# Masks written into the score banks by ScalarE, the up weights split as a seventh part, and new orders and banks in a six-layer local-attention kernel

## The reference

```python
x = attn_layer(shift_tokens(x), Wqkv[i], ...) + x     # 16 heads of 64, windows of 32 tokens
x = ffn_layer(shift_tokens(x), ln_g[i], ..., W1[i], b1[i], W2[i], b2[i]) + x

# attn_layer
q, k, v = split(x @ Wqkv)                  # 128 -> 3 * 1024
q, k = l2norm(q) * qs, l2norm(k) * ksc     # then a rotation by position, scaled
sim = einsum(q, k of this window and the one before) * 8
sim = where(mask, -big, sim)               # mask = (it < jb) | (it > jb + w) | (jb == -1)
return (softmax(sim) @ v) @ Wo
# ffn_layer
xn = layernorm(x) * g + b;  a, gate = split(xn @ W1 + b1)    # 128 -> 2 * 341
return a * gelu(gate) @ W2 + b2
```

## Time and profile before

| | us |
|---|---|
| median of 3 runs | 1497.31 (1495.83 to 1497.71) |
| the profiled execution | 1497.48 |
| its span | 1495.7 |
| PE busy | 1449.7 (97%) |
| DVE busy | 1348.3 (90%) |
| ACT busy | 1275.3 (85%) |
| POOL busy | 1245.6 (83%) |

### The profile page before, as it was taken

The page is one execution under the profiler, slowest core; times in us unless marked ns, Lnnn a source line. Parts: engine busy times, 40 slices in busy tenths (PEclk is TensorE's granted clock), DMA queues, the critical chain, the costliest instruction groups (busy, mean ns, idle before and its releaser), DMA issues.

```text
span 1495.7 us, 67060 instructions
## 1 busy us (share of the span) xinstructions
PE 1449.7 (97%) x26608; PEld 1290.8 (86%) x26608; DVE 1348.3 (90%) x2418; ACT 1275.3 (85%) x2605; POOL 1245.6 (83%) x1214
## 2 busy tenths in 40 slices
PE   6699999999999999999999999999999999999997
PEld 5578898889888888888898888889888988988886
DVE  7699999999999999999999999999999999999974
ACT  4577988888888898898889888888988888888886
POOL 5489988888899889898888898888889888888871
PEclk9999999999999999999999999999999999999999
DMA  6111122111122211221211122121212111211211
GB/s 162 43 42 50 49 59 63 45 49 53 47 54 66 70 37 40 62 63 51 76 43 41 49 57 74 53 61 35 59 36 65 44 45 40 56 49 35 52 46 28
DMA packets 96187, 80.31 MB, mean 54 GB/s; under 512 B 66282, under 2 KB 79598, under 8 KB 95854
## 3 DMA queue, kind: packets, MB, share of 16 engines
q1 hardware_dynamic: 94990, 75.34, 18.8%
q10 hardware_dynamic: 864, 0.26, 0.1%
HBM read 17.91 MB, written 1.05 MB: 13 GB/s over the span
## 4 chain that ended last, share of the span: by engine, by line
PE 88%; issue 4%; DVE 3%; ACT 3%; POOL 1%; DMA 1%; SPq 0%; ACTq 0%; POOLq 0%; DVEq 0%
PE bank L1140 70%; PE bank L1254 11%; PE bank L1292 5%; PE bank L1224 1%; ACT pz L725 1%; DVE parts L944 1%; PE bank L1326 1%; DMA rot<-in_b_v 0%; ACT sq L663 0%; ACT ot L732 0%; DVE n L954 0%; DVE w_lo L1026 0%; DVE s L990 0%; POOL rot L487 0%; POOL rot L476 0%
## 5 line engine op out<-in xcount | busy, mean ns | idle before, releaser
L476 POOL TENSOR_TENSOR rot<-parts 128x512 f32<-128x512 f32 x384 | 492.1, 1288 | 35.4 <-DVE parts L944 33.4
L944 DVE TENSOR_TENSOR parts<-bank,rtab 128x1024 f32<-128x1024 f32 x384 | 458.7, 1200 | 7.7 <-ACT sq L663 7.4
L487 POOL TENSOR_TENSOR rot<-rot,rnorm 128x512 f32<-128x512 f32 x384 | 394.6, 1043 | 12.0 <-DVE rnorm L970 12.0
L493 POOL TENSOR_TENSOR es<-es,r 128x512 f32<-128x512 f32 x192 | 200.4, 1044 | 151.8 <-DVE r L996 151.7
L954 DVE TENSOR_REDUCE n<-sq 128x8 f32<-128x512 f32 x384 | 259.1, 675 | 16.5 <-ACT sq L663 16.5
L1140 PE MATMUL bank<-w_hi,x_hi 128*128 128x512 f32 x576 | 265.6, 461 | 4.0 <-DVE parts L944 2.6
L663 ACT ACTIVATE sq<-bank 128x512 f32<-128x512 f32 x384 | 232.1, 604 | 18.5 <-PE bank L1140 6.9
L725 ACT ACTIVATE pz<-bank 64x512 f32<-64x512 f32 x384 | 225.9, 588 | 5.4 <-PE bank L1292 1.9
L1140 PE MATMUL bank<-w_lo,x_hi 128*128 128x512 f32 x576 | 228.5, 397 | 0.0
L1140 PE MATMUL bank<-w_hi,x_lo 128*128 128x512 f32 x576 | 228.0, 396 | 0.0
L1254 PE MATMUL bank<-ident,rot 128*128 128x128 f32 x1536 | 208.5, 273 | 10.7 <-DVE x_tok L1040 5.0
(11 more groups left out here) (95 smaller groups left out, 2901.9 us busy)
## 6 DMA issues: line engine op xcount, KB each, us to landing
vb<-v SPq DMA_DIRECT2D x96, 384.0 KB, 4.4
w_new<-in_Wqkv SPq DMA_DIRECT2D x36, 256.0 KB, 4.0
vb<-v SPq DMA_DIRECT2D x48, 128.0 KB, 2.3
w_o<-in_Wo SPq DMA_DIRECT2D x12, 256.0 KB
xin<-x_tok SPq DMA_DIRECT2D x48, 64.0 KB
xs<-x_tok SPq DMA_DIRECT2D x48, 64.0 KB, 2.0
xin<-x_tok SPq DMA_DIRECT2D x48, 56.0 KB
xs<-x_tok SPq DMA_DIRECT2D x48, 56.0 KB, 2.3
```

What stands on the lines that cost most here:

```text
L476: g.tensor_tensor(rot[:, i * CH:(i + 1) * CH].rearrange(halves, z=2, c=HD), parts[:, b:b + CH].rearrange(halves, z=2, c=HD), parts[:, b + ...
L487: g.tensor_tensor(c, c, over(r, CHH, DH), ALU.mult).then_inc(s_sc[i], 1)
L493: g.tensor_tensor(e, e, over(r8[:, (u % 2) * PAIRS:(u % 2 + 1) * PAIRS], PAIRS, DH), ALU.mult)\
L944: d.tensor_tensor(parts[:, b:b + 2 * CH].rearrange("p (w h c) -> p w h c", w=2, c=DH), heads(bank[QK_BANK[i]][:, :]).unsqueeze(1).to_broad ...
```

## The change

It has four parts.

1. The eight mask products of each `scores` go. In their place ScalarE copies the mask, now f32, from SBUF into the two score banks before the score products (`seed`, four instructions of 128 x 512 in a step), and the score products accumulate onto it. Before the pipeline starts, TensorE runs one product of 512 columns into each of the banks 2 and 3. Both `S_BANK` entries now use the banks 2 and 3.
2. The up weights are a seventh part in the same chain as the six of `Wqkv`: `next_hi` on ScalarE and `next_lo` on GpSimd, in the seventh of a layer's eight steps that split. `w_new` holds two parts of `Wqkv` by turns and the up weights apart; `w1_hi` and `w1_lo` hold two layers. `up_hi`, `up_lo` and their semaphores go.
3. The order inside `iteration` is new on all five engines, and the banks are new.
4. `align_block` is at the head of TensorE's iteration, with slot 24.

The core of the diff (the written-out orders are shown as they come out of the build below):

```diff
-QK_BANK, T_BANK = (2, 1, 2, 5, 1, 2, 5, 7), (0, 0, 7, 3, 6, 5, 4, 7)
-V_BANK, P_BANK, O_BANK = (3, 6, 5, 0), (4, 6, 7, 4), (2, 6, 7, 4)
-S_BANK, W_BANK, H_BANK = ((6, 3), (3, 1)), (3, 5), (6, 7, 4)
-XIN_BANK, N_BANK, D_BANK = 0, 4, 0
+QK_BANK, T_BANK = (7, 6, 3, 5, 4, 2, 1, 3), (0, 0, 5, 4, 7, 6, 7, 0)
+V_BANK, P_BANK, O_BANK = (2, 5, 1, 0), (7, 1, 7, 1), (5, 6, 4, 4)
+S_BANK, W_BANK, H_BANK = ((2, 3), (3, 2)), (4, 6), (0, 5, 6)
+SEEDED = (2, 3,)
+XIN_BANK, N_BANK, D_BANK = 6, 4, 1
...
-        w_new = sb("w_new", QKV)
+        w_new = sb("w_new", 2 * CH + 2 * HID)
...
+        def chunk(l, c):
+
+            if c < WCH:
+                return slice((c % 2) * CH, (c % 2 + 1) * CH), slice((l % 2) * QKV + c * CH, (l % 2) * QKV + (c + 1) * CH)
+            return slice(2 * CH, 2 * CH + 2 * HID), slice((l % 2) * 2 * HID, (l % 2 + 1) * 2 * HID)
...
             def split_lo(l, c):
-                pool.wait_ge(s_wh, l * WCH + c + 1)
...
+                pool.wait_ge(s_wh, l * WPARTS + c + 1)
+                new, w = chunk(l, c)
+                hi, lo = (w_hi, w_lo) if c < WCH else (w1_hi, w1_lo)
+                g.tensor_tensor(lo[:, w], w_new[:, new], hi[:, w].bitcast(F32), ALU.subtract).then_inc(s_wl, 1)
...
+            def seed(n, T, b):
+
+                first = 128 * int(T == 0 and b == 1)
+                a.activation(bank[S_BANK[T][b]][:, :].rearrange("p (h c) -> p h c", h=PAIRS // 2),
+                             mask[:, first:first + 128].unsqueeze(1).to_broadcast([P, PAIRS // 2, 128]), ACT.Copy)\
+                 .then_inc(s_seed[T], 1)
...
-            def up_lo(n):
-
-                if n % SEQS == SEQS - 1 and layer(n) < DEPTH - 1:
-                    dve.wait_ge(s_uph, layer(n) + 2)
-                    d.tensor_tensor(w1_lo[:, :], w_new[:, 0:2 * HID], w1_hi[:, :].bitcast(F32), ALU.subtract)\
-                     .then_inc(s_upl, 1)
...
+            for b in SEEDED:
+                mm(bank[b][:, :], ident[:, :], w_o[:, 0:CH])
...
+            def scores(n, T):
+
+                for i in range(4 * T, 4 * T + 4):
+                    pe.wait_ge(s_qte[i], done(n))
+                pe.wait_ge(s_seed[T], 2 * n + 2)
+                for half in range(PAIRS // 2):
...
-                for odd in range(2):
-                    for hh in range(2):
-                        for b in range(2):
-                            first = 128 * int(T == 0 and b == 1)
-                            r, o = 64 * hh, 64 * odd + 32 * (hh ^ b)
-                            mm(bank[S_BANK[T][b]][o:o + WIN, :], identh[r:r + DH, r:r + WIN],
-                               mask[r:r + DH, first:first + 128].unsqueeze(1).to_broadcast([DH, PAIRS // 2, 128]),
-                               stop=False)
-                score_heads(n, T, range(PAIRS // 2)).then_inc(s_s[T], 1)
...
-                    align_block(8)
...
+                    align_block(24)
```

More of the change, by code:

```diff
@@ L29 @@
 WCH = QKV // CH
+WPARTS = WCH + 1
 MASKED = -1.0e30
@@ L335, in _ @@
                     weights(l, part)
-            up_weights(0)
-            for c in (2, 3, 4, 5, 0, 1):
+            for c in range(2, WCH):
+                qkv_weights(0, c)
+            for c in range(2):
                 qkv_weights(1, c)
+            up_weights(1)
             def shifted(n, dst, signal):
@@ L616, in split_hi @@
                     last = (l - 1) * SEQS - 1
+                    if c == WCH:
+                        for j in range(HCH):
+                            act.wait_ge(s_hid[j], done(last))
                     for k in range(2):
@@ L712, in half_square, with freed @@
                  .then_inc(s_half[T], 1)
+            def freed(*uses):
+                for signal, n, *place in uses:
+                    if live(n):
+                        act.wait_ge(signal, upto(place[0], n, place[1]) if place else done(n))
+                        return
+            def seed(n, T, b):
[3 more added lines that the diff above has]
+                 .then_inc(s_seed[T], 1)
             def exps(n, u):
@@ L846, in iteration @@
                 if live(n - 1):
+                    first_root(n - 1, 1)
                     half_square(n - 1, 1)
+                if live(n):
+                    square(n, 2)
+                if live(n - 1):
+                    copy_v(n - 1, 1)
+                    take_qk(n - 1, 3)
+                if live(n - 2):
+                    take_p(n - 2, 2)
+                if live(n - 1):
+                    copy_v(n - 1, 0)
+                if live(n):
+                    square(n, 3)
+                if live(n - 1):
+                    freed((s_v[0], n - 1))
+                    seed(n - 1, 0, 0)
+                    freed((s_rot[0], n, 8, 2), (s_rot[1], n - 1, 8, 7))
+                    seed(n - 1, 0, 1)
             for n in range(STEPS + DEEP):
@@ new lines, in iteration @@
+                if live(n - 4):
+                    xg_lo_part(n - 4)
+                if live(n):
+                    rotate(n, 0)
+                if live(n - 5):
+                    finish(n - 5)
+                if live(n - 1):
+                    newton_half(n - 1, 1)
+                    newton_root(n - 1, 1)
+                if live(n):
+                    rotate(n, 1)
+                if live(n - 3):
+                    stats(n - 3)
+                if live(n):
+                    squares(n, 1)
+                    rotate(n, 2)
+                    squares(n, 2)
+                    squares(n, 3)
+                    rotate(n, 3)
@@ new lines, in iteration @@
+                if live(n - 2):
+                    freed((s_qte[1], n - 2))
+                    project_v(n - 2, 3)
+                if live(n - 1):
+                    freed((s_v[1], n - 2))
+                    project(n - 1, 3)
+                if live(n - 3):
+                    freed((s_rot[1], n - 1, 8, 1), (s_mid[1], n - 4), (s_qte[5], n - 3))
+                    values(n - 3, 1)
+                    freed((s_qte[3], n - 2), (s_xg, n - 5), (s_ot[3], n - 4))
+                    values(n - 3, 2)
```

501 lines of the change are left out of this document (210 added, 291 removed).

## The result

| | before | after |
|---|---|---|
| median, us | 1496.99 (1495.83 to 1497.71, 4 runs) | 1479.98 (1478.02 to 1482.22, 4 runs) |
| ratio | | 0.9888, interval 0.987 to 0.9905 |
| the profiled execution, its span | 1497.48, 1495.7 | 1482.22, 1480.4 |

A forecast was written before the change was run, and what follows sets the result against it. The prediction took TensorE's own work, 29.2 us a step, as the bound. From 1497.5 us it took 24.2 (masks and tiles) and 6.5 (ends of layers), and added 3.5 (waits on ScalarE): 1470.3 us, range 1460 to 1493.

The forecast's parts named there:

- the forecast's mechanism: TensorE's own sum sets the pace at 28.65 us a step, busy over 99%, with ScalarE's list just fitting; chance 0.63.
- the first two rivals: ScalarE sets the pace mildly, 1484 us, chance 0.16; or seeds in ScalarE's queue make it slower, 1509 us, chance 0.10.
- Masks: On TensorE, removing the mask products saves their spacing of 0.23 us per pass of scores, 0.46 us a step.
- Tiles: On TensorE, fewer turns between small tiles and whole-array work save 0.09 us a step, with ends at -0.09 and +0.14.
- What ScalarE gets: Four mask copies a step at 0.53 us each add 2.1 us, giving ScalarE 28.1 us of work in 28.65.
- it closes at 28.5 to 28.7: ScalarE's list, with two short waits, comes round in that many us a step, leaving TensorE 0.08 us of waits.
- the first rival, the mild pace of ScalarE: 0.4 us a step of ScalarE's old waits stay, making the step about 28.95 us and the time 1484; chance 0.16.
- Ends of layers: The five long steps lose their whole excess, 5 x (30.5 - 29.2) = 6.5 us, lower end 5.0.
- Start and end, "at zero": The pipeline's start and end cost nothing, with 5 us either way, since `take_in` to `down` stays five steps.
- Seeds in ScalarE's queue, slower: On ScalarE, seeds at 0.65 us and 1.0 us of forced waits make the step 29.6 us, time 1509; chance 0.10.
- Late stream: The shifted stream reaches VectorE's `stats` late by DMA, costing 0.4 us a step, 18 us more, 1488; chance 0.07.
- Instruction supply: On TensorE, the moved aligned place adds 0.2 us to each pass of scores, 18 us more, 1488; chance 0.04.

The follow-up runs named there:

- b_no_masks: The kernel before with the eight mask products of each pass of scores left out and nothing in their place: 1473.98 us, ratio 0.9842.
- x_mask_slot0: The changed kernel with mask products back on TensorE in place of ScalarE's copies, and the `align_block` slot 0 instead of 24: 1481.8 us, ratio 0.9905.
- x_no_seed: The changed kernel with its four mask copies a step left out and nothing in their place: 1461.31 us, ratio 0.9768.
- x_newton_one_input: The changed kernel with VectorE's first Newton instruction, which reads two inputs, replaced by one that reads a single input: 1473.17 us, ratio 0.9837.
- x_hi_moved: The changed kernel with ScalarE's `next_hi` moved to just before the fourth square of the next sequence: 1476.12 us, ratio 0.9856.
- x_hi_between: The changed kernel with ScalarE's `next_hi` moved to before the third square of the next sequence: 1465.8 us, ratio 0.9796.
- b_up_pool: The kernel before with the low part of the up weights computed by GpSimd, behind `next_lo`, instead of VectorE: 1491.79 us, ratio 0.9958.
- x_hi_between_pool: The changed kernel with `next_hi` before the third square and both Newton instructions moved from VectorE to GpSimd: 1465.05 us, ratio 0.9795.
- x_slot56: The changed kernel with TensorE's `align_block` slot at 56 instead of 24: 1564.56 us, ratio 1.0457.

## Why the prediction was right, and where it was not

The time is in the range, and the sign and its reason hold: the mask products have left TensorE and the long steps at ends of layers are gone. By its own signs, though, the forecast's mechanism did not come, and that 1479.98 still lies just inside its own range of 1460 to 1480 is luck: TensorE is busy for 98.8% and not over 99%, `take_in` recurs every 28.95 us and not every 28.6 to 28.8, and TensorE waits for a seed in 28 of some 34 steps, which was the sign of the first two rivals.

The forecast of 1470.3 stands beside 1482.2 of the profiled execution, 11.9 us off, and this is where they are. In the 41 steps I had 41 x 0.47 + 6.5 = 25.8 us saved and 21.1 were. At start and end I had 1.4 saved and 5.8 were lost.

**Masks.** Right in kind and a little small: 0.46 us a step said, 0.55 shown by `b_no_masks`, which counts 0.11 that the second scores themselves got shorter. In the new order the products are worth 0.40 (28.82 of `x_mask_slot0` against 28.42 of `x_no_seed`).

**Tiles.** 0.09 said, with ends to 0.14. `b_no_masks` leaves the old order with 28.60 and `x_no_seed` the new one with 28.42: 0.18. The turn from values to scores costs about 0.1 instead of my 0.05; what I had missed is that scores followed by a whole-array product need 1.40 us, and the 1.62 of the earlier trace rows went with the masks and the transpose behind them. TensorE's sum is 28.45 (28.65 said), 41 x 0.20 = 8.2 us better than the forecast.

**What ScalarE gets.** The size was right: 0.53 a seed said, 0.55 measured, and 968.5 us of work over 34.6 steps are 28.0 us a step (28.1 said).

**The step that failed: "it closes at 28.5 to 28.7", and 0.08 us a step for what that leaves.** It closes at 28.95. The waits are 28.87 - 28.45 = 0.42 us a step on average, 41 x 0.34 = 13.9 us worse. (8.2 better, 13.9 worse, and 1.0 better because the old steps add up to 1204.7 us and not to 36 x 29.2 + 5 x 30.5 = 1203.7, leave the 25.8 - 21.1 = 4.7.) This is the first rival, the mild pace of ScalarE, given 0.16, with a step of 28.95 and 1484; its numbers were the better ones, but by luck. Its terms, 28.1 + 0.2 + 0.4, make 28.7 and not 28.95; and I got them from a remainder of ScalarE's old waits, where the cause is the ring of `exps`, `newton_half` and `squares`. I had followed VectorE only for the seed of the second pass, and for the rest laid ScalarE's list beside TensorE's. TensorE waits at the first pass. Its ring goes over VectorE, and through an instruction that I counted among the short ones by its size, where the kernel before already has it with 1.17 us in one of its two places:

```profile
722.51 1.17 DVE L963 SCALAR_TENSOR_TENSOR newton<-n2c,half_sq 128x32 f32<-128x32 f32 x1
```

`x_newton_one_input`, `x_hi_moved` and `x_hi_between` show the ring; the forecast's mechanism is the one that `x_hi_between` has, and there it gives 1465.8.

**Ends of layers.** Right: 6.5 said, 6.0 by `b_up_pool`, and no step of 30.5 us is left after the change. GpSimd's part of 682 columns takes 1659 ns (the most of this row; 1669 in the earlier trace rows) and no engine is shown waiting for it. The step of the wide part is up to 0.24 us longer than its neighbours: 0.15 is `next_hi`, 0.78 us there and 0.63 elsewhere, and about 0.1 stands in `x_no_seed` too, where no seed waits, and is not explained.

```profile
L467 POOL TENSOR_TENSOR w_lo<-w_new,w_hi x42: 1270/1298/1659, 21.7 to 1177.3; 128x512 fp32r<-128x512 f32 x36, 128x682 fp32r<-128x682 f32 x6
```

**Start and end, "at zero": failed.** "The depth from `take_in` to `down` stays five steps" is true of iterations and not of time: within the iteration `take_in` moved forward and `down` did not follow, 4.3 us. All nine other kernels with the new order end 99.0 to 102.2 us after their last `take_in`, and the other three with the old one 91.7 to 92.6 (93.3 in the kernel before). So the 6 us belong to the order, and it could have been read from it. That the other 2 us come from idle time between the stages of the drain I have not shown.

**The rivals.** *Seeds in ScalarE's queue, slower*: it did not come; the seeds overlap with their neighbours (1.18 us for the two of a row, and the next instruction starts 1.11 behind the first). *Late stream*: `stats` waits for no DMA between 300 and 1300 us in the kernel after, although a landing takes more than before (2.1 in the earlier trace rows):

```profile
DMA to landing us min/median/max: 2.0/2.5/3.2
```

The margin is as thin as said: in `x_hi_between_pool`, with a faster VectorE, the wait appears, at no cost to the time.

```profile
DVE stat L1019 <- DMA xs<-x_tok: 22.4, 36, 1.0
```

*Instruction supply*: not in the kernel after, and given 0.04 because no row of before showed it. The runs show that this was too little, and my 0.2 us for each pass too: one argument makes 9, 36 and 85 us. Of waits of PE by issue between 300 and 1300 us the new order has none with slot 24, one of 1.2 us with slot 8, and with slot 56 the 65 of 0.3 to 1.8 us; with mask products it has 37 of at most 1.0 us (20.6 in all) with slot 24, and two of 1.5 with slot 0. That these waits are the supply of instructions is inferred: one argument moves them, nobody is waited for, and no trace shows that anything happens at a multiple of 256 instructions. Which property of the place decides, I leave open. Nearly all of the waits stand within small-tile products or, the larger ones of `x_slot56` and all of `b_slot24`, seven to eleven whole-array products and transposes behind a long row of them; but slot 24 was not shown to keep clear of such places in the new order.

**What each part is worth.** Ends of layers 6. Masks to ScalarE as placed: 1480 against 1481.8 with the products kept, about nothing, since 0.4 us of waits replace 0.4 us of products. The rest, some 8 us, is the order with its banks and slot (1495.9 to 1481.8, less the 6), the longer drain included. With `next_hi` moved, taking the masks from TensorE is worth the further 16 us (1481.8 to 1465.8).

## What to carry to other kernels

When work moves to an engine with slack, do not only sum its list: follow each ring over all engines that hand a buffer on, with the durations in the rows and not those that sizes suggest, and look at the steps in which one piece is missing; a step that is shorter without it shows the ring and where it closes. A single movable piece then often fits between two rings. After any change in the number of small matmuls, try a few alignments before judging the change, and read the length of the drain from the order, as the distance between first and last stage within an iteration.

## What I had not expected of the hardware

- The argument of `align_block` moves this kernel from 1480 us (24) to 1565 (56), with nothing else changed; the profile shows it only as idle time ended by issue (55.7 us of 1000 there). The waits on other engines grow with it and mislead: those of `sq` on ScalarE for TensorE are 2.6 us of the 1000 in the kernel after and 41.9 in `x_slot56`.
- A VectorE instruction of 32 columns took 1.16 us beside a GpSimd instruction that read SBUF, and 0.19 us for its like alone; with the first of the two made to read one input, the wait went to the second, 0.95 us.
- Score products of 64 x 32 tiles take 1.39 to 1.41 us before values or a whole-array product (1.45 behind a wait), 1.51 before a transpose, and 1.62 with masks ahead and a transpose behind.
